# Two 8-dimension heads per 32-row quarter of a PSUM bank, and engine orders from a list scheduler with amounts added per step

## What is computed

```
x = x + tanh(g0) * attention(LN(x), context; 8 heads of 64, Wq, Wk, Wv, Wo, bo)          # stage X
x = x + tanh(g1) * ( self_attention(LN(x); 16 heads of 8, W_qkv)                         # stage F
                     + sum over the top 2 of 8 experts of gate * (LN(x) @ We + be) )
x = x + tanh(g2) * attention(LN(x), context; 16 heads of 8, Wq, Wkv, Wo, bo)             # stages K and B
x = x + tanh(g3) * (top 2 of 8 experts with normalised weights)(LN(x))                   # stage C
```

## Time and profile before

| | |
|---|---|
| Median of the runs | 752.5 us |
| The profiled execution | 746.59 us, of which the span from first to last instruction is 744.8 us |
| Mean granted clock of PE over the span | 0.933 of full |
| PE, weight loads of PE | busy 663.1 and 336.2 us |
| DVE, ACT, POOL | busy 569.7, 374.2 and 344.5 us |
| DMA | 40.8 MB moved, mean 55 GB/s |

### The profile page before, as it was taken

How to read it: one execution, slowest core, us unless ns; L and a number is a source line. 1 busy time by engine, 2 the same in 40 slices (tenths; PEclk the granted TensorE clock), 3 DMA queues, 4 the chain that set the end, 5 groups by cost and what they waited for, 6 DMA issues and landing times.

```text
span 744.8 us, 13302 instructions
## 1 busy us (share of the span) xinstructions
PE 663.1 (89%) x5232; PEld 336.2 (45%) x5232; DVE 569.7 (76%) x1055; ACT 374.2 (50%) x482; POOL 344.5 (46%) x467
## 2 busy tenths in 40 slices
PE   6699898998999899989999999989999789787684
PEld 2265454553544455434645355534653424333342
DVE  2626578589998879788898979887888987928534
ACT  4064345545546753775357644765357346263360
POOL 4273753852463257415663368326764324422233
PEclk9599999999999999989999999999999969969597
DMA  7210202112101221121121311121013221021000
GB/s 193 80 58 19 86 1 62 45 44 63 43 24 41 77 64 52 52 79 32 41 66 42 99 48 65 36 75 50 22 58 97 71 68 68 4 89 55 7 1 14
DMA packets 45790, 40.82 MB, mean 55 GB/s; under 512 B 4824, under 2 KB 37536, under 8 KB 45728
## 3 DMA queue, kind: packets, MB, share of 16 engines
q1 hardware_dynamic: 45168, 39.52, 17.1%
q10 hardware_dynamic: 560, 0.46, 0.2%
HBM read 22.93 MB, written 17.04 MB: 54 GB/s over the span
## 4 chain that ended last, share of the span: by engine, by line
PE 66%; DVE 21%; ACT 6%; issue 2%; POOL 2%; DMA 2%; SPq 1%; POOLq 0%; DVEq 0%
PE psum L670 13%; PE psum L626 7%; PE psum L590 7%; DVE mx8B L925 7%; PE psum L582 6%; DVE mxA L831 4%; PE psum L658 4%; ACT probB L740 4%; PE psum L557 3%; PE psum L639 3%; PE psum L551 3%; PE psum L600 2%; PE psum L577 2%; DVE rden L839 2%; PE psum L675 2%
## 5 line engine op out<-in xcount | busy, mean ns | idle before, releaser
L925 DVE TENSOR_REDUCE mx8B<-psum 128x2 f32<-128x1024 f32 x128 | 153.7, 1219 | 22.7 <-PE psum L639 21.5
L740 ACT ACTIVATE probB<-psum 128x1024 f32<-128x1024 f32 x128 | 126.4, 1029 | 57.2 <-PE psum L658 56.5
L727 ACT ACTIVATE probX<-psum 128x1024 f32<-128x1024 f32 x64 | 65.5, 1024 | 95.1 <-PE psum L582 94.8
L920 DVE TENSOR_REDUCE mx8F<-psum 128x4 f32<-128x1024 f32 x64 | 77.0, 1217 | 8.8 <-PE psum L633 8.6
L831 DVE TENSOR_REDUCE mxA<-psum 128x2 f32<-128x1024 f32 x64 | 76.6, 1216 | 8.5 <-PE psum L564 8.1
L839 DVE RECIPROCAL rden<-psum 128x256 f32<-128x256 f32 x32 | 56.1, 1752 | 34.8 <-PE psum L594 34.7
L740 ACT ACTIVATE probF<-psum 128x1024 f32<-128x1024 f32 x64 | 65.1, 1026 | 24.0 <-PE psum L658 22.2
L999 POOL TENSOR_TENSOR prodC<-prodC 128x256 f32<-128x256 f32 x30 | 21.8, 725 | 104.6 <-DVE prodC L913 102.3
L670 PE MATMUL psum<-probB,v8B 128*32 128x256 f32 x1024 | 67.5, 408 | 2.8 <-ACT probB L740 2.7
L582 PE MATMUL psum<-qX,kX 64*128 64x256 f32 x512 | 68.4, 388 | 0.0
L991 POOL TENSOR_TENSOR psum_k<-probX 128x512 f32<-128x512 f32 x32 | 40.8, 1274 | 59.5 <-ACT probX L727 58.5
(11 more groups left out here) (192 smaller groups left out, 1174.2 us busy)
## 6 DMA issues: line engine op xcount, KB each, us to landing
k8B<-k_dK SPq DMA_DIRECT2D x32, 192.0 KB
k_dK<-partsK SPq DMA_DIRECT2D x8, 384.0 KB, 2.5
q8F<-q_dF SPq DMA_DIRECT2D x32, 96.0 KB
k8F<-k_dF SPq DMA_DIRECT2D x32, 96.0 KB
q8B<-q_dB SPq DMA_DIRECT2D x32, 96.0 KB
k_dK<-partsK SPq DMA_DIRECT2D x8, 256.0 KB, 2.7
cTX<-in_ctxT SPq DMA_DIRECT2D x8, 192.0 KB, 2.8
cTK<-in_ctxT SPq DMA_DIRECT2D x8, 192.0 KB, 2.4
```

The costliest lines, as they stand in the source:

```text
L727: nc.scalar.activation(prob[s][(8 * b + k) % SLOTS[s]][:], ps, ACT.Exp, scale=float(XD) ** -0.5).then_inc(done["ACT"], 1)
L740: nc.scalar.activation(prob[s][(units * b + k) % SLOTS[s]][:], ps, ACT.Exp, scale=float(D8) ** -0.5).then_inc(done["ACT"], 1)
L920: nc.vector.tensor_reduce(mx8[s][:].rearrange("p t (i q) -> p i t q", i=2)[:, :, :, k], ps.rearrange("p (i t n) -> p i t n", i=2, t=QT), A ...
L925: nc.vector.tensor_reduce(mx8[s][:, t, :].rearrange("p (i q) -> p i q", i=2)[:, :, p], ps.rearrange("p (i n) -> p i n", i=2), AX.X, ALU.ma ...
```

## The change

**Packing.** In `pv8`, an even fill k and the odd fill k+1 now share one bank. The odd one's stationary operand starts 16 columns earlier, so that its head lands on rows 16 to 24 of the same quarter and adds zeros to rows 0 to 8; for that the tiles v8 hold zeros outside the 8 values and one column of ones. The odd fill starts no accumulation but goes on with that of the even one. One ACT instruction drains both, so there are two drains instead of four per batch and stage, oU has two parts, and `oT` has two transposes per half instead of four. The value columns and their biases are permuted on the host, and the query and key columns with them, so that the output heads come out in the right order. The even fill's drain waits for the odd fill on PE (`act.wait_ge(is_full(pv8, k + 1))`).

**The planner.** `more` adds a PE job with no drain of its own. `URGENT` adds an amount per stage and step to the length of way that breaks ties, `TURN` one per stage and batch. `NEAR` lets PE take, among the fills that could start within 0.15 us of its first possible one, the one with the longest way. A few durations are corrected (`sp` 3.9, 3.9, 2.2 to 3.1, 3.05, 1.95 us, `oT` on PE 0.55 to 0.30).

```diff
+URGENT = {
+    "X": {"kp": 1, "ln": -2, "out": -4, "rs": 5, "vp": 5, "xh": 1, "xin": 40},
+    "F": {"gate": 12, "mT8": 2, "mr": 21, "mx8": 2, "oT": 40, "qk": 10, "sr": -20, "sw": -5, "v8": -2, "xh": 7},
+    "K": {"ctx": 5, "kk": -2, "sp": -24, "sr": 20},
+    "B": {"aT": 40, "e8": 9, "ln": 20, "ls": -60, "mT8": 2, "mw": -2, "oT": -2, "rs": -10, "sp": -40, "sr": -40, "xh": -21},
+    "C": {"out": -4, "rs": 4, "xh": -2},
+}
+TURN = {"X": (2, 0, -10, 20, 5, 0, 0, -5), "F": (0, 0, -2, 0, 0, 2, 0, 0), "K": (0, 0, 0, 0, 0, 12, 20, 0), "B": (0, 0, 0, 0, 0, 0, 0, -10), "C": (0, 0, 0, 0, 0, 10, 0, 0)}
+NEAR = {"PE": 0.15}
...
+    def more(self, s, name, b, k, busy, pe=()):
+        self.drain[s, name, b, k] = None
+        self.job("PE", s, name, b, k, busy, *pe)
...
     for k in range(4):
-        p.fill("ACT", 0, s, "pv8", b, k, 1.0 if s == "F" else 1.87, .39, [("ACT", s, "e8", b, n * (k + 1) - 1), v], [("PE", s, "oT", b - 1, 1)])
+        work = 1.0 if s == "F" else 1.87, [("ACT", s, "e8", b, n * (k + 1) - 1), v]
+        if k % 2 == 0:
+            p.fill("ACT", 0, s, "pv8", b, k, work[0], .39, work[1], [("PE", s, "oT", b - 1, 1), ("PE", s, "pv8", b, k + 1)])
+        else:
+            p.more(s, "pv8", b, k, *work)
     for k in range(QT):
-        p.fill("DVE", 0, s, "oT", b, k, .55, .95 if s == "F" else .58, [("ACT", s, "pv8", b, 3)], old)
+        p.fill("DVE", 0, s, "oT", b, k, .3, .95 if s == "F" else .58, [("ACT", s, "pv8", b, 2)], old)
...
+    way = {key: us + URGENT.get(key[1], {}).get(key[2], 0) + TURN.get(key[1], (0,) * BATCH)[key[3]] for key, us in way.items()}
...
-                rank = start, -way[key]
-                if best is None or rank < best[0]:
-                    best = rank, key, banks
+                found.append((start, -way[key], key, banks))
+            if e in NEAR:
+                soon = min(one[0] for one in found) + NEAR[e]
+                one = min((one for one in found if one[0] <= soon), key=lambda one: (one[1], one[0]))
+            else:
+                one = min(found, key=lambda one: one[:2])
+            if best is None or one[:2] < best[0]:
+                best = one[:2], one[2], one[3]
...
-        oU = per("FB", "oU", [P, 4, SEQ])
+        oU = per("FB", "oU", [P, 2, SEQ])
...
-                            last = mm(ps[32 * i:32 * i + 32, 0:SEQ], v8[s][:, c, h, :], prob[s][(NPAIR * KEYS[s] // SEQ * b + u) % SLOTS[s]][:, o:o + SEQ],
-                                      start=(c == 0), stop=(c == n - 1), tile_position=(0, 32 * i))
+                            at = 32 * h - 16 * (k % 2)
+                            last = mm(ps[32 * i:32 * i + 32, 0:SEQ], v8[s][:, c, :, :].rearrange("p h d -> p (h d)")[:, at:at + 32], prob[s][(NPAIR * KEYS[s] // SEQ * b + u) % SLOTS[s]][:, o:o + SEQ],
+                                      start=(c == 0 and k % 2 == 0), stop=(c == n - 1 and k % 2 == 1), tile_position=(0, 32 * i))
                 elif name == "oT":
-                    pe.wait_ge(*is_done(s, "pv8", b, 3))
-                    for g in range(4):
+                    pe.wait_ge(*is_done(s, "pv8", b, 2))
+                    for g in range(2):
...
                 elif name == "pv8":
+                    act.wait_ge(*is_full(s, "pv8", b, k + 1))
                     act.wait_ge(*is_full(s, "oT", b - 1, 1))
-                    nc.scalar.activation(oU[s][:, k, :], ps[:, 0:SEQ], ACT.Copy).then_inc(done["ACT"], 1)
+                    nc.scalar.activation(oU[s][:, k // 2, :], ps[:, 0:SEQ], ACT.Copy).then_inc(done["ACT"], 1)
...
-                for tile in (k8["F"], v8["F"], v8["B"]):
-                    engine.memset(tile[:], 1.0).then_inc(c_set, 1)
+                engine.memset(k8["F"][:], 1.0).then_inc(c_set, 1)
+                for n, s in enumerate("FB"):
+                    engine.memset(v8[s][:], 0.0).then_inc(v_zero, 1)
+                    pool.wait_ge(v_zero, n + 1)
+                    engine.memset(v8[s][:, :, :, D8:D8 + 1], 1.0).then_inc(c_set, 1)
```

More of the change, by code:

```diff
@@ L142, in plan_f @@
     plan_gate(p, "F", b, (1.2, .95))
-    plan_stack(p, "F", b, 3.9, 6, ("ACT", "F", "qk", b, 0), ("F", "e8"))
+    plan_stack(p, "F", b, 3.1, 6, ("ACT", "F", "qk", b, 0), ("F", "e8"))
     p.fill("DVE", 0, "F", "v8", b, 0, .62, .43, [("ACT", "F", "ln", b, 0)], [("PE", "F", "pv8", b - 1, 3)])
@@ L154, in plan_k @@
     p.fill("ACT", 0, "K", "kk", b, 0, 1.0, 1.4, [("SP", "K", "ctx", b, 0)], [("SP", "K", "sw", b - 1, 0)])
-    plan_stack(p, "K", b, 3.9, 3, ("ACT", "K", "kk", b, 0), ("B", "e8"))
+    plan_stack(p, "K", b, 3.05, 3, ("ACT", "K", "kk", b, 0), ("B", "e8"))
     for k in range(2):
@@ L163, in plan_b @@
     p.fill("DVE", 0, "B", "qk", b, 0, .5, 1.0, [("ACT", "B", "ln", b, 0)], [("SP", "B", "sw", b - 1, 0)])
-    plan_stack(p, "B", b, 2.2, 3, ("DVE", "B", "qk", b, 0), ("B", "e8"))
+    plan_stack(p, "B", b, 1.95, 3, ("DVE", "B", "qk", b, 0), ("B", "e8"))
     plan_attend(p, "B", b, "KB", ("DVE", "K", "vv", b, 1), 2 * NPAIR,
@@ L227, in schedule @@
         for e, keys in could.items():
+            found = []
             for key in keys:
@@ L232, in schedule @@
                     drain = p.drain[fill], *fill
-                    if any(a not in over for a in jobs[drain][1] if a != key):
+                    if drain[0] and any(a not in over for a in jobs[drain][1] if a != key and p.drain.get(a[1:], "") is not None):
                         continue
-                    when, banks = free_banks(p.wide[fill], bank_free, start)
+                    when, banks = free_banks(p.wide[fill], bank_free, start) if drain[0] else (0., None)
                     if when >= never:
@@ L240, in schedule @@
                         start = max(start, free["DVE"] + line - LEAD - jobs[key][0])
-                rank = start, -way[key]
-                if best is None or rank < best[0]:
-                    best = rank, key, banks
+                found.append((start, -way[key], key, banks))
+            if not found:
+                continue
+            if e in NEAR:
[5 more added lines that the diff above has]
+                best = one[:2], one[2], one[3]
         (start, _), key, banks = best
@@ L252, in schedule @@
         if e == "PE":
-            before[fill] = [held[i] for i in banks if held[i]]
-            bank_of[fill] = banks[0]
-            for i in banks:
+            before[fill] = [held[i] for i in banks if held[i]] if banks else []
+            bank_of[fill] = banks[0] if banks else bank_of[fill[:3] + (fill[3] - 1,)]
+            for i in banks or ():
                 held[i], bank_free[i] = fill, never
@@ L403, in build @@
         w_keys, w_values, w_queries, w_ident, zeroed = sem("w_keys"), sem("w_values"), sem("w_queries"), sem("w_ident"), sem("zeroed")
+        v_zero = sem("v_zero")
         picked = sem("picked")
@@ L852, in _ @@
                 elif name == "oT":
-                    heads = ps.rearrange("p (h n) -> p h n", h=H8)
+                    heads = ps[:, 0:2 * P].rearrange("p (h n) -> p h n", h=H8)
                     if s == "B":
@@ L1025, with places @@
     g = {k: np.asarray(v) for k, v in inputs.items()}
+    def places(m):
+        return np.swapaxes(m.reshape(m.shape[:-1] + (2, 4, 2, D8)), -3, -2).reshape(m.shape)
     def dh(m):
-        return np.moveaxis(m.reshape(m.shape[:-1] + (NPAIR, 2, D8)), -3, -1).reshape(m.shape)
+        return np.moveaxis(places(m).reshape(m.shape[:-1] + (NPAIR, 2, D8)), -3, -1).reshape(m.shape)
     wqkv, bqkv = g["L0_ffn_W_qkv"], g["L0_ffn_b_qkv"]
@@ L1038 @@
         "boX": g["L0_xattn_bo"], "boB": g["L1_xattn_bo"],
-        "wq8F": dh(wqkv[:, :P]), "wk8F": dh(wqkv[:, P:2 * P]), "wv8F": wqkv[:, 2 * P:],
-        "bq8F": dh(bqkv[:2 * P].reshape(2, P)).T, "bv8F": bqkv[2 * P:],
-        "wq8B": dh(g["L1_xattn_Wq"]), "wk8B": dh(wkv[:, :P]), "wv8B": wkv[:, P:],
-        "bq8B": np.stack([dh(g["L1_xattn_bq"]), dh(bkv[:P])], axis=1), "bv8B": bkv[P:],
+        "wq8F": dh(wqkv[:, :P]), "wk8F": dh(wqkv[:, P:2 * P]), "wv8F": places(wqkv[:, 2 * P:]),
+        "bq8F": dh(bqkv[:2 * P].reshape(2, P)).T, "bv8F": places(bqkv[2 * P:]),
+        "wq8B": dh(g["L1_xattn_Wq"]), "wk8B": dh(wkv[:, :P]), "wv8B": places(wkv[:, P:]),
+        "bq8B": np.stack([dh(g["L1_xattn_bq"]), dh(bkv[:P])], axis=1), "bv8B": places(bkv[P:]),
         "wo8": g["L1_xattn_Wo"],
```

## The result

The changed kernel takes 758.46 us, the median of 20 runs (753.61 to 761.41), against 754.25 for the kernel before on the same chip (20 runs, 750.38 to 757.58). The ratio is 1.008 [1.0058, 1.0103]: 0.8% slower. The two medians by themselves give 1.0056, so a difference of 0.2 or 0.3% between two ratios means little. Executions more than 1.5% above the fastest of their kernel are left out of the ratios. The forecast was 727.5 us with a range to 756, so it was wrong in sign and size.

The account below looks back on a forecast made before the run. The prediction took PE to bound most of the span. Its terms, -7.0 - 1.3 + 3 + 0.4 - 20 = -24.9 us, took the profiled 746.6 to 721.7, a median of 727.5 against 752.5; range 704 to 756 us.

Parts of the forecast that it names:

- What bounds it: Whole kernel: PE bounds most of the span, busy 89% of it and holding 66% of the chain that ended last.
- Transposes, -7.0: oT on PE: 64 of 128 transposes go, 0.22 us saved in each of 32 fills, 7.0 us less.
- Drains, -1.3: pv8 drains on ACT: 32 of 64 go, almost none on the chain, 1.3 us less, bounds 0 and -12.3.
- rival 3: pv8 drains on ACT count in full, 11.0 us more saved: 716.5 us, chance 0.05.
- Banks, +3: Even pv8 fills hold their bank until the odd drain; planner places fills around it: 3 us more, bounds 0 and +40.
- Rival 5: Held banks in the middle make PE wait for drains, +16 us, no gain from the order: 760.6 us, chance 0.09.
- The start, +0.4: POOL's two more small memsets for v8, ahead of the second x's load: 0.4 us more, bounds 0.2 and 3.6.
- The order, -20: Planner's new amounts and choice within 0.15 us: 13 us less at the end, 4 for clock, 3 in the middle.
- Rival 1: The order brings nothing; the end stays a chain of three batches of B: 747.5 us, chance 0.14.
- Rival 4: Saved PE time becomes waiting, as DVE may set the pace in patches: 752 us, chance 0.05.

Follow-up runs that it names:

- the hold alone: Lists of the kernel before, banks given out anew, nothing packed, but each even pv8 fill's bank kept until the odd one's drain: 779.44 us, 1.0225 to before.
- the experiments on the start: POOL's larger memsets behind the first xb, second x loaded between weights: on the kernel before 1.0027, on the unpacked kernel with searched amounts 0.9733, both to before.
- replay, nothing packed: Fixed lists of the kernel before, banks given out anew by a function, v8 holding zeros, four drains and four transposes: 759.15 us, 1.0086 to before.
- the work saved alone: Kernel before with two of four transposes per oT fill left out: 750.49 us, 0.9965; then also without the odd pv8 drains: 748.03 us, 0.9926.

## Why the prediction was wrong, by its own steps

**What bounds it: held in part.** PE is the busiest engine, and 0.7% came from work taken off it and ACT. But the four largest rows of waits were read as the measure of bank shortage, and they are not: 7.4 us before and 7.7 after. The list scheduler orders steps around banks that are not free, so a shortage goes into the order. Planned with ten banks instead of eight (planned only, not run), the kernel before would end at 741.7 us instead of 756.2.

**Transposes, -7.0: mis-sized.** Shown: -2.6 (0 to -5.4) where -7.0 stood. The pitch was right. The timeline of PE in after at a fill of two, beside the earlier trace rows:

```profile
207.54 0.44 PE L705 MATMUL psum<-ident,oUF 128*128 128x128 f32 x2
207.91 0.39 PE L606 MATMUL psum<-mrow,pick 64*128 64x512 bf16 x2
```

0.37 us, as forecast. But an instruction's pitch is the work that it takes from PE, not what the end gains; the lower bound of the working, 4.6 by the chain's share, was nearer.

**Drains, -1.3: near.** Shown: -2.9 as the difference of two ratios, inside the bounds 0 to -12.3. The Trainium skill (TensorEngine Tiling (Array Packing), "PSUM Bottleneck") says that emptying the banks may become the bottleneck; then they would have counted in full. The groups of after, beside the earlier trace rows:

```profile
L774 ACT ACTIVATE oUB<-psum 128x256 f32<-128x256 f32 x16 | 6.2, 387 | 17.2 <-PE psum L700 17.1
L774 ACT ACTIVATE oUF<-psum 128x256 f32<-128x256 f32 x16 | 6.1, 384 | 12.7 <-PE psum L700 12.7
```

Half of them are gone, 12.3 us of ACT's work, and about a quarter of that reached the end. So emptying the banks was not what set the pace, and rival 3 falls. The same section of the Trainium skill advises to empty several tiles of one bank in one access. Here that did not pay, since two tiles filled 7 us apart hold their bank for all of that time.

**Banks, +3: the step that failed first.** It was priced by the nearest row of small waits, on the ground that the planner would place fills around the held bank. Shown: about 11 us in the changed kernel, and in the old order 1.4% (the hold alone) to 3.1% (by subtraction), 10 to 24 us; the bounds 0 and +40 hold it, the +3 does not. Rival 5 had the mechanism, with a chance of 0.09. That its 760.6 us is so close to the 758.5 measured is in part luck: it has 7.0 for the transposes, where 2.6 were shown, and +16 for the banks, where about 11 were. Its sign, over 20 us of waits of L658 and L639 in the middle, was set wrong: the same sum is 10.5 us in before, 11.0 in after and 15.1 in the packed kernel with the old order, and passes 20 (22.2) only in the kernel that is 5% slower.

**The start, +0.4: right for POOL, and of no account.** The timeline of POOL and SP in after, beside the earlier trace rows:

```profile
9.23 3.12 SPq L526 DMA_DIRECT2D wq8B<-in_wq8B  x1
...
10.98 0.15 POOL L987 MEMSET v8F<- 128x32 f32 x1
...
12.90 0.21 POOL L987 MEMSET v8B<- 128x64 f32 x1
...
14.32 0.72 POOL L1016 TENSOR_TENSOR xbX<-xin,boX 128x256 f32<-128x256 f32 x1
...
15.92 0.38 SPq L480 DMA_DIRECT2D xin<-in_x  x1
```

`xb` began at 13.94 in before and 14.32 here, +0.38. The load of the second x came 1.17 us later and the first maxima's scores 1.7 us later (25.44), since SP had also spent 3.12 us on one issue. In the experiments on the start, moving it moved nothing at the end.

**The order, -20: the step that failed worst.** -13 for the end, -4 for clock and -3 for the middle rested on a bound ("as dense as the middle") and a share of 40% with no row behind it. The new rules on the unpacked kernel gave 1.0009, +0.7 us. On the packed one the choice and the amounts were worth over 4%, which only compensated. The corrected durations had no term at all, though in the plan they alone cost the unpacked kernel 11 us. A gain of the size forecast was there to be had, 0.9733 for the unpacked kernel with searched amounts, but these amounts did not bring it. Rival 1 was right about the order but had the hold at +3.

**The sum as shown.** -2.6 for the transposes, -2.9 for the drains, about +11 for the banks and +0.7 for the order come to the +6 us that the ratio of 1.008 stands for, where the sum had -24.9. The banks' share is what is left over between two measured kernels, so that the sum closes is no proof of it; that it agrees with the hold alone is the support.

**Rival 4** (the saved PE time turns into waiting) describes the account of after in part: idle time grew. But PE did not get less busy. And the cause is the bank; the saved work did count where nothing was held.

**What would have told it.** The kernel contains its own planner, and the end of the plan that it makes when it is built can be read off without a chip. Set beside the medians (us):

```
kernel                                   plan's end   measured
before                                      756.2       754
after                                       764.3       758.5
packed, old order                           773.3       776.8
unpacked, new rules                         758.9       752.4
replay, nothing packed                      758.2       759.2
packed F only / B only                   764.3 / 769.3  762.4 / 772.5
hold alone, nothing packed                  777.2       779.4
packed, no amounts, no choice               792.6       792.6
packed, choice within 0.15 us               770.7       771.2
packed / unpacked, searched amounts      745.9 / 734.5  745.1 / 733.2
```

Every sign outside the noise is right and no error in this table is above 7 us. The two kernels of "the work saved alone" are missing from it: they cut steps out after the plan is made, so their plan is that of before. The plan's end tells of one list, not of a rule. With HOP, a constant of the plan, at 0.06 or 0.08 us instead of 0.07, the plan of before ends at 766.1 or 768.9 us. With ten banks, the packed kernel's plan with the choice but without amounts ends at 736.6 us and the unpacked one's at 744.5; with neither, at 746.5 and 737.6. So whether packing would pay with more banks depends on the rule of choice. All this was only planned, not run.

**What stays open.** The hold's exact size in the old order: the two ways to it differ by 1.7% with wide intervals, and what else packing might cost there (the merged drain in ACT's list, for one) was not tested by itself. The unpacked kernel with the corrected durations alone was not run. Holding only where no stage wants pairs was not tried, nor a kernel that fills the two halves of a shared bank directly after each other.

## What to carry to other kernels

Merging the drains of two fills pays with instructions and costs with bank time. Multiply the extra hold by what it blocks (here a pair, since wide fills need both neighbours), and judge it by the share of all bank pairs, not only by the few largest rows of waits. Where a static order comes from a list scheduler, run that scheduler on the change first: here the largest waits in the trace hid the scarcity, and the end of the plan did not. And when a change brings new work and new ordering rules together, try the rules on the old kernel too: searched anew for the unpacked kernel, amounts (with the corrected durations) gave 2.7%.

## What was not expected of the hardware

**One program, several clocks.** Executions of one kernel differ by up to 2%: the kernel before ran between 745.4 us, at a granted clock of 0.935, and 759.6, at 0.916, in 29 runs; the packed one with the old order between 773.7 at 0.915 and 780.6 at 0.905. So a part of what separates two executions goes with the clock. An example is "packed, old order" beside "work saved alone", with the same counts of instructions on PE and ACT: spans 776.9 and 741.4 us, idle 102.3 and 83.3, clock 0.906 and 0.926. 19.0 us of the difference is idle time; the other 16.5 us is PE's busy time (674.6 against 658.1) for the same matmuls at a lower clock. In this pair more waits went with a lower clock, and together they cost nearly twice the idle time. It is one pair of executions, in two orders, and which of the two drove the other is not shown.

**Busy time does not count work.** After has 64 transposes fewer than before and 2.3 us more of PE busy time, at 0.923 against 0.933.

**An issue of varying length.** The DMA issue of wq8B held SP for 3.12 us in after and for 0.71 in before, with the same bytes. What it waited for the profile does not show.
